# First attention of a two-layer image tower: scores transposed and split by image, two heads' keys on 76 partitions, values carried by transfers, one mask on VectorE

## What is computed

```python
q = proj(Wq) * d ** (-0.5)
k = proj(Wk)
v = proj(Wv)
s = jnp.einsum('bhqd,bhkd->bhqk', q, k)
attn = 1.0 + s + 0.5 * s * s
causal = jnp.tril(jnp.ones((t, t), dtype=bool))
attn = jnp.where(causal, attn, 0.0)
o = jnp.einsum('bhqk,bhkd->bhqd', attn, v)
z = jnp.sum(attn, axis=-1, keepdims=True) + EPS
o = o / z
y = o.transpose(0, 2, 1, 3).reshape(b, t, dim)
return y @ Wo.T
```

## Time and profile before

| | |
|---|---|
| runs | 285.54, 285.22, 284.0 us; median 285.22 |
| span of the profiled execution | 284.1 us |
| TensorE matmul busy | 250.1 us (88%), weight load 197.7 us (70%) |
| VectorE busy | 182.9 us (64%) |
| ScalarE busy | 152.0 us (54%) |
| GpSimd busy | 157.2 us (55%) |
| mean granted TensorE clock | 0.988 |
| chain that ended last | TensorE 58%, VectorE 26%, issue 6%, ScalarE 5% |

### The profile page before, as it was taken

One profiled execution on the slowest core, in us unless ns is written; L12 is line 12 of the kernel. 1 busy time (PEld: TensorE's weight loads), 2 busy tenths in 40 slices (PEclk: granted clock), 3 DMA queues, 4 the chain that ended last, 5 costly groups with the idle time before them and its releaser, 6 DMA issues.

```text
span 284.1 us, 8057 instructions
## 1 busy us (share of the span) xinstructions
PE 250.1 (88%) x3292; PEld 197.7 (70%) x3292; DVE 182.9 (64%) x347; ACT 152.0 (54%) x322; POOL 157.2 (55%) x227
## 2 busy tenths in 40 slices
PE   0779989957999899897997899999999997988983
PEld 0667878845888688686886788888888884434331
DVE  0534628511559999999998588988777785534111
ACT  1312102056898868776765166675657653833450
POOL 7441324544374988787889556868676661145000
PEclk9999999999999999999999689999999999999999
DMA  5899430000000000000000000000000000002021
GB/s 176 202 248 310 106 98 0 3 0 0 3 2 2 0 2 2 2 2 3 3 2 0 2 2 2 3 3 2 3 2 5 2 3 2 0 0 68 0 66 44
DMA packets 9897, 9.81 MB, mean 35 GB/s; under 512 B 4303, under 2 KB 9030, under 8 KB 9862
## 3 DMA queue, kind: packets, MB, share of 16 engines
q1 hardware_dynamic: 9446, 9.31, 12.1%
q10 hardware_dynamic: 416, 0.01, 0.1%
HBM read 8.07 MB, written 1.25 MB: 33 GB/s over the span
## 4 chain that ended last, share of the span: by engine, by line
PE 58%; DVE 26%; issue 6%; ACT 5%; DMA 2%; POOL 2%; ACTq 0%; DVEq 0%; POOLq 0%
PE psum L1262 11%; PE psum L1298 7%; PE psum L1462 5%; PE psum L1445 5%; DVE img L1025 4%; DVE big L1018 4%; PE psum L1545 4%; PE psum L1520 3%; PE psum L1608 3%; PE psum L1596 3%; PE psum L1234 3%; DVE st L979 2%; PE psum L1535 2%; DMA w_raw<-in_L_tok_W 2%; DVE xq L1066 2%
## 5 line engine op out<-in xcount | busy, mean ns | idle before, releaser
L1298 PE MATMUL psum<-hnT,a 128*128 128x114 f32 x352 | 49.2, 284 | 1.6 <-ACT mT L695 1.2
L1298 PEld LDWEIGHTS psum<-hnT,a 128*128 128x128 f32 x352 | 44.0, 195 | 5.8 <-issue 2.1
L464 POOL TENSOR_SCALAR ve<-mvs 114x1 f32<-114x1 f32 x44 | 18.6, 422 | 52.1 <-DVE mvs L981 50.7
L1262 PE MATMUL psum<-wT,patchT 128*114 128x256 f32 x132 | 33.0, 405 | 1.6 <-DVE patchT L935 0.8
L459 POOL TENSOR_SCALAR big<-mT,parmask 128x228 f32<-128x228 f32 x22 | 22.8, 1047 | 20.9 <-ACT mT L665 20.9
L465 POOL TENSOR_TENSOR rstd<-ve,nhalf 114x1 f32<-114x1 f32 x44 | 27.8, 631 | 3.7
L485 POOL TENSOR_TENSOR big<-big,img 114x912 f32<-114x912 f32 x11 | 22.4, 2039 | 12.3 <-ACT big L729 12.3
L1262 PEld LDWEIGHTS psum<-wT,patchT 128*114 128x114 f32 x132 | 24.4, 191 | 7.0 <-DVE patchT L935 2.1
L1018 DVE SCALAR_TENSOR_TENSOR big<-big,img 114x912 f32<-114x912 f32 x11 | 17.5, 1590 | 14.8 <-ACT big L719 14.8
L719 ACT ACTIVATE big<-psum 114x912 f32<-114x912 f32 x22 | 19.3, 928 | 6.1 <-PE psum L1344 5.9
L979 DVE BATCH_NORM_STATS2 st<-h_all 114x6 f32<-114x256 f32 x44 | 18.8, 428 | 1.5
(11 more groups left out here) (156 smaller groups left out, 557.6 us busy)
## 6 DMA issues: line engine op xcount, KB each, us to landing
img<-in_x SPq DMA_DIRECT2D x6, 576.0 KB, 10.1
out<-h_all SPq DMA_DIRECT2D x10, 114.0 KB
w_raw<-in_L_tok_W SPq DMA_DIRECT2D x1, 768.0 KB, 5.9
a_raw<-in_L_attn_Wq SPq DMA_DIRECT2D x1, 256.0 KB, 8.5
a_raw<-in_L_attn_Wk SPq DMA_DIRECT2D x1, 256.0 KB, 8.6
a_raw<-in_L_attn_Wv SPq DMA_DIRECT2D x1, 256.0 KB, 8.7
a_raw<-in_L_attn_Wo SPq DMA_DIRECT2D x1, 256.0 KB, 11.9
qw<-in_L_ffn_weight SPq DMA_DIRECT2D x1, 256.0 KB, 12.0
```

The source lines that it names most:

```text
L464: step(nc.gpsimd.tensor_scalar(ve[:, t:t + 1], mvs[:, t, 1:2], LN_EPS, None, ALU.add))
L1262: last = nc.tensor.matmul(EB[t % 2][0:T, 0:D], patchT[:, c, FIRST[t]:FIRST[t] + TI, :].rearrange("p b s -> p (b s)"), wT[:, c, :], start=( ...
L1298: return nc.tensor.matmul(bk[:, m * T:(m + 1) * T], w[:, c, m * 128:(m + 1) * 128], hnT[:, c, :], start=(c == 0), stop=(c == DC - 1))
```

## The change

The scores are laid out anew. Scores are taken by image: a matmul has the 38 queries of one image as moving columns and, as stationary matrix, the keys of both heads of a pair, 2 x 38 = 76 columns (kX, which holds k twice, each time with one head of the pair set to zero). Keys of the even head land on partitions 0 to 37, of the odd head on 38 to 75. scores0 has 24 matmuls; the four banks hold 228 columns each, 912 in all on 76 partitions, and one square reads them. add_one and GpSimd's mask are gone; one VectorE instruction adds one and masks all 912 columns with maskP. values0 has 24 matmuls (76 keys, 32 output rows, 38 columns) and needs no accumulation; sums0 has 8 of 114 columns with oneP. The two scaled copies are made of k instead of q.

values0 wants the values of an image with both heads' keys on partitions 0 to 75. take_v0 now writes rows of the tile (vS, two buffers, odd heads 16 columns further) and SyncE carries them with six transfers per tile (three images, two parities, 38 rows of 1 KB each) into vB0, in a new loop between its loads and its stores. take_v0(t) waits for the transfers of tile t-2, the transfers of t for values0(t-2), values0(t) for all six.

On GpSimd the memsets of vX and vX2 (114 x 2304 each) become one of vS (114 x 1088), and maskT and oneX become maskP, maskO and oneP (three memsets, five selects, one sum), with the same count of constants.

```diff
-        vX = sb("vX", [T, H * (128 + HD)])
+        vS = sb("vS", [T, 2, 2 * D + 2 * HD])
...
-        vX2 = [vX, img_[0:T, 0:H * (128 + HD)]]
-        at = H * (128 + HD)
-        qX = img_[:, at:at + 2 * DC * T].rearrange("p (c o t) -> p c o t", c=DC, o=2)
-        at += 2 * DC * T
+        KK = 2 * S
+        vB0 = [img_[0:KK, n * TI * D:(n + 1) * TI * D].rearrange("p (i n) -> p i n", i=TI) for n in range(2)]
+        at = 2 * TI * D
+        kX = img_[:, at:at + DC * TI * KK].rearrange("p (c i k) -> p (c i) k", c=DC, i=TI)
+        at += DC * TI * KK
...
-        oneX = img_[0:T, at:at + 3 * HD]
-        maskT = img_[0:T, at + 3 * HD:at + 3 * HD + T]
-        eps0 = img_[:, at + 3 * HD + T:at + 3 * HD + T + 1]
-        E3 = [big[0:T, n, :].rearrange("p (h t) -> p h t", h=H) for n in range(3)]
+        oneP = img_[0:KK, at:at + 2 * HD]
+        maskP = img_[0:KK, at + 2 * HD:at + 2 * HD + T]
+        eps0 = img_[:, at + 2 * HD + T:at + 2 * HD + T + 1]
+        maskO = img_[0:KK, at + 2 * HD + T + 1:at + 2 * HD + 2 * T + 1]
+        E3 = [big[0:KK, n, 0:H // 2 * T].rearrange("p (m t) -> p m t", m=H // 2) for n in range(3)]
...
-        e_pool = sem("e_pool")
+        v_moved = [sem("v_moved0"), sem("v_moved1")]
...
             for t in range(NT):
+                sp.wait_ge(lay[0]["v_sb"], t + 1)
+                ge(sp, lay[0]["oT_ps"], t - 1)
+                for i in range(TI):
+                    for o in range(2):
+                        sp.dma_start(vB0[t % 2][o * S:(o + 1) * S, i, :], vS[i * S:(i + 1) * S, t % 2, o * D:(o + 1) * D]
+                                     ).then_inc(v_moved[t % 2], 16)
+            for t in range(NT):
...
-            nc.gpsimd.memset(vX[:, :], 0.0).then_inc(consts, 1)
+            nc.gpsimd.memset(vS[:, :, :], 0.0).then_inc(consts, 1)
...
             pool.wait_ge(by_patch_dve, 2)
             pool.wait_ge(by_patch_act, 1)
-            nc.gpsimd.memset(vX2[1][:, :], 0.0).then_inc(consts, 1)
...
-            def mask_weights(t):
-                pool.wait_ge(lay[0]["ex"], 2 * t + 2)
-                e = E3[t % 3][:, H // 2:H, :]
-                nc.gpsimd.tensor_tensor(
-                    e, e, maskT[:, :].rearrange("p (o t) -> p o t", o=1).to_broadcast([T, H // 2, T]), ALU.mult
-                    ).then_inc(e_pool, 1)
             def round_to_grid(p):
...
             def layer0():
...
-                mask_weights(0)
...
                 for t in range(NT):
...
-                    if t + 1 < NT:
-                        mask_weights(t + 1)
...
                 act.wait_ge(L["m_ps"], t + 1)
...
-                nc.scalar.activation(mT[:, :, :], KQ0[:, 0:DC * T].rearrange("p (c t) -> p c t", c=DC), ACT.Copy
-                                     ).then_inc(L["m_sb"], 1)
+                for o in range(2):
+                    last = nc.scalar.activation(kX[:, :, o * S:(o + 1) * S],
+                                                KQ0[:, 0:DC * T].rearrange("p (c s) -> p c s", s=S), ACT.Copy,
+                                                scale=parmask[:, o:o + 1])
+                last.then_inc(L["m_sb"], 1)
...
             def take_q0(t):
...
                 act.wait_ge(L["s_ps"], t + 1)
...
-                for o in range(2):
-                    last = nc.scalar.activation(qX[:, :, o, :], KQ0[:, 0:DC * T].rearrange("p (c t) -> p c t", c=DC),
-                                                ACT.Copy, scale=parmask[:, o:o + 1])
-                last.then_inc(L["s_sb"], 1)
+                nc.scalar.activation(mT[:, :, :], KQ0[:, 0:DC * T].rearrange("p (c t) -> p c t", c=DC), ACT.Copy
+                                     ).then_inc(L["s_sb"], 1)
...
             def take_v0(t):
...
                 act.wait_ge(L["v_ps"], t + 1)
-                ge(act, L["oT_ps"], t - 1)
-                nc.scalar.activation(vX2[t % 2][:, :].rearrange("p (h q) -> p h q", h=H)[:, :, 0:HD],
-                                     VB0[0:T, :].rearrange("p (h d) -> p h d", h=H), ACT.Copy).then_inc(L["v_sb"], 1)
+                ge(act, v_moved[t % 2], 16 * 2 * TI * (t // 2))
+                rows = vS[:, t % 2, :].rearrange("p (o n) -> p o n", o=2)[:, :, 0:D]
+                nc.scalar.activation(rows.rearrange("p o (m q) -> p o m q", m=H // 2)[:, :, :, 0:HD],
+                                     VB0[0:T, :].rearrange("p (m o d) -> p o m d", o=2, d=HD), ACT.Copy
+                                     ).then_inc(L["v_sb"], 1)
...
             def square(t):
...
                 act.wait_ge(L["sc"], t + 1)
...
-                for n in range(2):
-                    last = nc.scalar.activation(
-                        E3[t % 3][:, n * (H // 2):(n + 1) * (H // 2), :].rearrange("p (r h) t -> p r (h t)", r=2),
-                        psum[0:T, n * 1024:(n + 1) * 1024].rearrange("p (r n) -> p r n", r=2)[:, :, 0:4 * T],
-                        ACT.Square, scale=HD ** -0.5, bias=1.0)
-                    last.then_inc(L["ex"] if n == 0 else squared, 1)
-            def add_one(t):
-                L = lay[0]
-                act.wait_ge(squared, t + 1)
-                e = E3[t % 3][:, H // 2:H, :]
-                nc.scalar.activation(e, e, ACT.Identity, bias=1.0).then_inc(L["ex"], 1)
+                nc.scalar.activation(
+                    E3[t % 3][:, :, :].rearrange("p (r c) t -> p r (c t)", r=4),
+                    psum[0:KK, 0:2048].rearrange("p (r n) -> p r n", r=4)[:, :, 0:DC * T],
+                    ACT.Square, scale=HD ** -0.5, bias=1.0).then_inc(squared, 1)
...
             def take_z(t):
...
-                add_one(0)
...
-                    if t + 1 < NT:
-                        add_one(t + 1)
...
             def mask_weights(t):
...
-                dve.wait_ge(lay[0]["ex"], 2 * t + 1)
-                e = E3[t % 3][:, 0:H // 2, :]
+                dve.wait_ge(squared, t + 1)
+                e = E3[t % 3]
...
-                    out=e, in0=e, scalar=1.0, in1=maskT[:, :].rearrange("p (o t) -> p o t", o=1).to_broadcast([T, H // 2, T]),
+                    out=e, in0=e, scalar=1.0,
+                    in1=maskP[:, :].rearrange("p (o t) -> p o t", o=1).to_broadcast([KK, H // 2, T]),
...
             def divide(t):
...
-                ge(pe, L["ex"], 2 * t)
+                ge(pe, squared, t)
                 for c in range(DC):
-                    for r in range(4):
-                        last = nc.tensor.matmul(bank[r][0:T, c * 2 * T:(c + 1) * 2 * T], mT[32 * r:32 * r + 32, c, :],
-                                                qX[32 * r:32 * r + 32, c, :, :].rearrange("p o t -> p (o t)"),
-                                                start=True, stop=True)
+                    for i in range(TI):
+                        for r in range(4):
+                            at = c * T + i * S
+                            last = nc.tensor.matmul(bank[r][0:KK, at:at + S], kX[32 * r:32 * r + 32, c * TI + i, :],
+                                                    mT[32 * r:32 * r + 32, c, i * S:(i + 1) * S], start=True, stop=True)
                 last.then_inc(L["sc"], 1)
...
             def values0(t):
...
-                pe.wait_ge(e_pool, t + 1)
-                pe.wait_ge(L["v_sb"], t + 1)
+                pe.wait_ge(v_moved[t % 2], 16 * 2 * TI * (t // 2 + 1))
...
                 for c in range(DC):
-                    for odd in range(2):
+                    for i in range(TI):
...
-                            at = (c * HC + 2 * r + odd) * (128 + HD) - HD * odd
-                            last = nc.tensor.matmul(OB0[32 * r:32 * r + 32, c * T:(c + 1) * T],
-                                                    vX2[t % 2][:, at:at + 32], E3[t % 3][:, (r * DC + c) * 2 + odd, :],
-                                                    start=(odd == 0), stop=(odd == 1))
+                            at, m = c * T + i * S, c * 4 + r
+                            last = nc.tensor.matmul(OB0[32 * r:32 * r + 32, at:at + S],
+                                                    vB0[t % 2][:, i, 2 * HD * m:2 * HD * (m + 1)],
+                                                    E3[t % 3][:, r * DC + c, i * S:(i + 1) * S], start=True, stop=True)
                 last.then_inc(L["oT_ps"], 1)
...
             def sums0(t):
                 for c in range(DC):
-                    for odd in range(2):
-                        for r in range(4):
-                            last = nc.tensor.matmul(ZB0[32 * r:32 * r + 32, c * T:(c + 1) * T],
-                                                    oneX[:, HD * (1 - odd):HD * (1 - odd) + 32],
-                                                    E3[t % 3][:, (r * DC + c) * 2 + odd, :],
-                                                    start=(odd == 0), stop=(odd == 1))
+                    for r in range(4):
+                        last = nc.tensor.matmul(ZB0[32 * r:32 * r + 32, c * T:(c + 1) * T], oneP[:, :],
+                                                E3[t % 3][:, r * DC + c, :], start=True, stop=True)
```

22 lines of the change are left out of this document (14 added, 8 removed).

## The result

| | kernel before | changed kernel |
|---|---|---|
| median of 4 runs each, us | 285.38 (284.0 to 289.16) | 276.35 (274.97 to 279.38) |
| profiled execution: span, mean clock | 284.1, 0.988 | 273.9 (time 275.67), 1.000 |

The ratio is 0.967, with a 95% interval of 0.960 to 0.973. The ratio leaves out the slowest run of each kernel (289.16 and 279.38), which fell into a slow state; without them the medians are 285.22 and 275.67. By the medians of the table 9.0 us are off, where 8.3 was forecast. The median lies within 0.6 us of the forecast of 276.9, but errors of opposite sign had a part in that. First the page of the changed kernel: span, the busy table, the slices of TensorE, VectorE, the granted clock and the moved GB/s, and the share of the chain by engine.

A forecast was written before the change was run, and what follows sets the result against it. VectorE was taken to bound layer 0 from tile 3's mask, TensorE the turns before. Gains 2.0 + 0.6 + 4.75 + 0.95 = 8.3 us cut the span from 284.1 to 275.8; plus 1.1, 276.9 (range 274.8 to 278.5).

The forecast's parts named there:

- (a): Start of layer 0: shorter ScalarE work brings scores0(1) to 68.0 instead of 70.02, a gain of 2.0 us.
- the overshoot: Layer 0, q_proj0 waiting for k's longer scaled copy: 0.1 to 0.4 us late.
- (b): Layer 0, turns 0 and 1: loop turns of 6.45 us gain 0.3, ScalarE being free 0.3 more.
- (c): Layer 0 from tile 3's mask: without GpSimd's mask, VectorE's lock-stretched instructions in turns 3, 5, 7, 9 shrink by 4.75 us.
- a rounding of about 1.27 takes its place: Turn 9: GpSimd's rounding replaces its mask of 1.96, so VectorE's wait shrinks by an estimated 0.9 us.
- (d): Turn 10: GpSimd's bias comes 1.96 earlier, so VectorE's subtraction takes about 0.8 instead of 1.75: 0.95 us.
- the signs that the prediction named: Layer 0: no mask above 2.2 us, VectorE not idle over 1 us, six issues within 3, TensorE never waiting for transfers.
- At nothing: the transfers: Layer 0: SyncE's six value transfers per tile, 6 to 7 us from copy to arrival, covered and costed at nothing.
- The rival with this mechanism: Layer 0: value transfers taking over 12 us from copy to arrival set the turn; 290 us, chance 0.06.
- the upper bound of 15 us: Value transfers, copy to arrival, if landing is three times as long; turn then 9.25 us.
- 9 us of cover: Time between a later tile's value copy and its use by TensorE, at turns of 6.45 us.
- the clock stays up: Rival, change of layers: TensorE's fall to 0.50 clock, costing 3 us, does not occur; 273.9 us, chance 0.15.

The follow-up runs named there:

- e4: Kernel before with GpSimd's mask left out, so the second half of the heads stays unmasked, nothing else changed: 278.86 us, ratio 0.978.
- e1: Changed kernel plus a GpSimd operation of about 2 us on a scratch tile in the old place of its mask: 282.82 us.
- e12: Changed kernel run once more with no edit: 276.17 us, ratio 0.969 to the kernel before.
- e6: Changed kernel with unused matmuls filling TensorE's hole at the change of layers, two before and one behind: 276.20 us.
- e11: Changed kernel with eight transfers per tile instead of six, the extra two into a scratch tile, TensorE waiting for all: 281.77 us.
- e3: Changed kernel with each of the six transfers per tile issued twice, the second into scratch, TensorE waiting for all twelve: 310.32 us.
- e10: Changed kernel with layer 0's first normalisation ahead of ScalarE's first weight part and GpSimd's bias add moved to even turns: 275.92 us.
- e2: Changed kernel with ScalarE's add of one given back on a scratch buffer: 277.96 us, ratio 0.973 to the kernel before.
- e5: Kernel before with unused matmuls filling TensorE's hole at the change of layers, three before and one behind: 284.03 us, ratio 0.996.
- e7: Changed kernel with GpSimd's bias add moved from odd turns to even turns: 276.21 us, ratio 0.968 to the kernel before.
- e8: Changed kernel with GpSimd's bias add moved to even turns and unused matmuls filling TensorE's hole at the change of layers: 275.69 us.
- e9: Changed kernel with layer 0's first normalisation issued ahead of ScalarE's first weight part: 275.06 us, ratio 0.964 to the kernel before.

## Why the prediction was right, and where it was not

Where both profiles have the fall of the clock, 7.8 us stand against the forecast's 8.3. Of the forecast's 8.3, 0.3 was to be won ahead of scores0(0), so in layer 0 its 8.0 stand against 7.0 to 7.2: the mechanism was right, and its terms add up to about 1 us too much. Point by point, with the first profile of the new kernel:

**(a) The start**, 2.0: measured 1.7. The order of events was right. The key copy of tile 0 ends at 61.97 and holds q_proj0(0) until 62.02, 0.24 later than before (61.78). This is the overshoot that the prediction named under ScalarE and left out of the sum.

**(b) Turns 0 and 1**, 0.6: measured 0.53. The turn of 6.45 us was 6.46 and 6.38. The price of the small matmuls of scores was right, 0.95 (0.96 start to start). Values took 0.46 instead of 0.62 and sums 0.51 instead of 0.45, 0.1 less together. The Trainium skill ("TensorE: Matmul & The Clock Gate", section "Wait — 56ns, not 53.3ns?") has some 25 ns from one matmul to the next at the least; 48 records in 0.96 us are 20 ns each. The trace doesn't agree, as in layer 1's values.

**(c) The lock**, 4.75: measured 4.3. Its mechanism is shown from both sides (e4, e1): 1.65 each was forecast for turns 5 and 7, and the trace has 1.6 and 1.8. Turn 3 gave 0.6, the 0.55 of the sum, though it looks otherwise in the trace. The bias (93.75) holds up the mask and not the product, and mask and product take 1.6 us less than before; but VectorE stands idle 1.00 us ahead of the reciprocal of tile 3, since TensorE made a pause inside sums0(3) and ScalarE's z came late:

```profile
90.99 0.58 PE L1366 MATMUL psum<-big,img 76*32 76x114 f32 x11 [1.21 <-issue]
```

Most of this pause was for free: a mask at 93.02 would have found GpSimd in its rounding until 93.75 (92.53, 1.27) and the bias behind it. One term was mis-sized. In turn 9 0.9 was expected, and 0.3 came (0.5 in e12 and e6, where the mask takes 1.92 and 1.91). The step that failed is "a rounding of about 1.27 takes its place, and the wait shrinks by 0.9". GpSimd's expansion waited for ScalarE, and the rounding began together with the mask:

```profile
137.97 1.72 POOL L476 TENSOR_SCALAR big<-mT,parmask 128x228 f32<-128x228 f32 x2 [1.04 <-ACT mT L671]
139.66 1.27 POOL L503 TENSOR_TENSOR qa<-qa,qc 114x512 f32<-114x512 f32 x1
```

```profile
139.71 2.18 DVE L1016 SCALAR_TENSOR_TENSOR big<-big,img 76x912 f32<-76x912 f32 x1
...
143.16 0.88 DVE L1080 COPY_PREDICATED sm<-keep,psum 114x608 f32<-114x608 int32 x1 [0.26 <-PE psum L1458]
```

GpSimd's date had been shifted by its own saving alone, without asking what it waits for. Here it waits, by way of ScalarE's copies, for TensorE, which pauses for 1.05 us inside sums0(9) (135.71). In e12 and e6 that pause is 0.78, and the mask is shorter by the same 0.27. Even in e4, where there is no such pause, the mask takes 1.97, so the 0.9 was too much in any case.

**(d) Turn 10**, 0.95: the subtraction took 0.79, as said, but 0.26 of it went into a wait for layer 1's scores(0) (143.16), which the prediction had "about even". 0.6 was left. Of the signs that the prediction named, no mask is above 2.18 us and VectorE is never idle for over 1.00 us between the mask of tile 3 and that of tile 9. Two others went against it, both about the transfers: TensorE did wait for one, and SyncE's six issues took 3.8 us, not 3.

**At nothing: the transfers.** In the sum this was about right, 0.3 us at the start (0.38 and 1.02 in e12 and e6) against "at most 1". The price of an issue was not: 0.57 to 0.68 us instead of 0.31 to 0.5, taken from a transfer of another form. Landing was right by luck: the 3.7 us of a small transfer and the 3.8 us here have nothing in common, since the landing grows with the number under way (3.8, about 5.4 and 6.0 us for the last of six, eight and twelve). The rival with this mechanism was the nearest one to coming true: with two transfers more it costs 5.6 us (e11); the upper bound of 15 us is near the 13 that twelve take (e3). "9 us of cover" was about right, but a chance of 0.06 was low for a way that takes 7.1 of them.

**The clock.** The forecast took the fall at the change of layers as fixed and only moved. It is not fixed. Over the profiled executions of one and the same kernel it was there once (e12) and once not, and of the profiles of the variants only e10 has one near the change of layers. e3 has seven, from 73 us on. The others have theirs at 60 to 65 (e2, e4, e5, e7, e8), 71 to 76 (e4, e11), 89 to 100 (e2, e9, e10, e11) and 113 to 144 (e1), or nowhere (e6). They are not equal. The one at the change of layers lasts 6.8 us before and in e12, 10.3 in e10, while each of the earlier ones, e3's aside, lasts 3.4. The 2.65 us were measured for one of 6.8. One of 3.4, at 60 to 64, makes scores0(0) 1.1 to 1.4 us late, counted from the end of the embedding (6.8 us in the two profiles of the new kernel and e6, 7.9 to 8.2 in e2, e7 and e8). The rival that put falls into layer 0 thus came up in some executions of the variants, with smaller falls than it had assumed. So "the clock stays up" was no rival to the forecast but a part of each run's luck, in the kernel before too: of its 37 runs beside the experiments three have a mean clock of 1.00, with 283.1 to 283.3 us; of the new kernel's ten runs four have it, with 274.3 to 275.7. The means of these groups, 283.2 and 274.8, lie 8.3 apart. (A mean clock of 1.00 doesn't fix the time: one run of e5 has it with 285.45.) What decides where in a run it falls stays open. Filling the hole at the change of layers didn't change the new kernel's time (e6), and on the kernel before it brought 1.1 us at the edge of the noise (e5).

**The metric.** I set the metric 1.1 us above the span, from the median; each execution's own time lies 1.7 to 1.8 above its span. That made the forecast 0.6 low, and the 0.5 that the pair with a fall fell short of 8.3 makes it 0.5 lower still. Put right in both it would be 278.0, and e12's execution with the fall took 278.06. Yet the median is 276.35, since it lies 9.0 under the median of before where the two profiles with a fall lie 7.8 apart. So it is luck that forecast and median lie only 0.6 us apart. That the new kernel has fewer or shorter low stretches in its median run fits: the median of the mean clocks is 0.994 over its ten runs and 0.985 over the 37 before, and 19 of the 37 lie below 0.988, none of the ten. That this makes the further 1.2 us wasn't shown.

## What to carry to other kernels

When two engines share a lock, cost each of their operations with the neighbour it will meet at the new pace, and follow the chain of waits of the other engine too, since its date doesn't move by its own saving. When small transfers replace computing, count the issue of each and treat the landing as growing with the number under way. Compare the rate at which they move with the length of a turn; six of them here cost nothing but 0.3 to 1.0 us at the start, eight cost 5.6 us. Where the clock falls in most runs, at a place that changes from run to run, take two profiles of each kernel, and compare those with the same falls, before a single stretch is credited to a change.
